# The last batch's output path as a program of its own, with folded context products

## The reference

```python
# layer 0: 16 heads of width 16
q = ln(x; ln1) @ q_w + q_b;  k = ctx @ k_w + k_b;  v = ctx @ v_w + v_b
hidden = softmax(q k^T / 4, masked) v @ cproj_w + cproj_b + x
y = gelu_tanh(ln(hidden; ln2) @ fc_w + fc_b) @ proj_w + proj_b      # inner width 1024
h = hidden + y
# layer 1: one head of width 256, over the same context
s = (h w_q^T) (ctx w_k^T)^T / 16
out = h + alpha * (softmax(s) (ctx w_v^T)) w_o^T
```

## Time and profile before

| | |
|---|---|
| median of 3 runs | 351.56 us |
| the profiled execution: its time | 353.57 us |
| the profiled execution: span from first to last instruction | 351.8 us |
| busy in the span: PE, DVE, ACT, POOL | 282.2, 217.2, 190.3, 93.0 us |
| iterations of batches 1 and 2 | 67.5 us each |
| iteration of batch 3, up to the last product with the values | 47.8 us |
| from there to the end | 60.3 us |

### The profile page before, as it was taken

One profiled execution on the slowest core, in us unless ns is written; L12 is line 12 of the kernel. 1 busy time (PEld: TensorE's weight loads), 2 busy tenths in 40 slices (PEclk: granted clock), 3 DMA queues, 4 the chain that ended last, 5 costly groups with the idle time before them and its releaser, 6 DMA issues.

```text
span 351.8 us, 5962 instructions
## 1 busy us (share of the span) xinstructions
PE 282.2 (80%) x2053; PEld 202.6 (58%) x2053; DVE 217.2 (62%) x420; ACT 190.3 (54%) x350; POOL 93.0 (26%) x88
## 2 busy tenths in 40 slices
PE   3671869985988998998979899989879888586765
PEld 2450436842336675764856576658467656386654
DVE  4541785466666859876488688665758532627432
ACT  3441264288546587767365959655385862225330
POOL 2152000312100267640022774200237140015200
PEclk9995698788789999999999999999999999967898
DMA  6129993019127107401730190053200000000000
GB/s 188 16 62 182 126 318 107 2 45 132 59 68 122 38 17 112 109 2 46 89 122 0 45 153 26 0 103 61 89 2 1 2 0 2 30 0 2 0 2 30
DMA packets 21485, 22.06 MB, mean 63 GB/s; under 512 B 2388, under 2 KB 18600, under 8 KB 21464
## 3 DMA queue, kind: packets, MB, share of 16 engines
q1 hardware_dynamic: 20024, 18.37, 27.8%
q10 hardware_dynamic: 1440, 3.41, 2.7%
HBM read 11.02 MB, written 1.05 MB: 34 GB/s over the span
## 4 chain that ended last, share of the span: by engine, by line
PE 34%; issue 26%; ACT 11%; POOL 11%; DVE 11%; DMA 4%; SPq 1%; ACTq 0%; POOLq 0%; DVEq 0%
PE post_ps L463 10%; PE post_ps L467 4%; PE om L535 4%; DVE neg_max L1042 3%; PE pre_ps L450 3%; POOL y_l L1343 3%; PE s L508 3%; PE s L525 2%; POOL ft L1338 2%; ACT probs L810 2%; ACT q_stack L801 2%; DMA k_stack<-kp 2%; PE post_ps L586 2%; POOL ln L1283 1%; ACT y_h L824 1%
## 5 line engine op out<-in xcount | busy, mean ns | idle before, releaser
L1042 DVE TENSOR_REDUCE neg_max<-s 128x1 f32<-128x512 f32 x128 | 83.3, 684 | 26.2 <-PE s L508 25.5
L810 ACT ACTIVATE probs<-s 128x512 f32<-128x512 f32 x128 | 75.3, 598 | 29.4 <-PE s L525 28.6
L508 PE MATMUL s<-k_stack,q_stack 97*128 97x512 bf16 x128 | 49.5, 410 | 22.9 <-DMA k_stack<-kp 14.7
L525 PE MATMUL s<-q_stack,k_stack 109*128 109x256 bf16 x256 | 50.5, 281 | 2.9 <-ACT q_stack L801 2.1
L508 PEld LDWEIGHTS s<-k_stack,q_stack 97*128 97x128 bf16 x128 | 12.3, 98 | 49.4 <-DVE neg_max L1042 25.6
L535 PE MATMUL om<-probs,vals 128*17 128x256 f32 x512 | 35.4, 397 | 0.7 <-ACT probs L810 0.7
L525 PEld LDWEIGHTS s<-q_stack,k_stack 109*128 109x128 bf16 x256 | 20.9, 101 | 17.1 <-ACT probs L810 3.8
L1283 POOL TENSOR_TENSOR ln<-ln,minus_half 128x2 f32<-128x2 f32 x8 | 5.6, 704 | 94.3 <-DVE ln L1006 94.3
L1068 DVE TENSOR_TENSOR y_l<-post_ps,y_h 128x512 fp32r<-128x512 f32 x16 | 10.9, 690 | 31.2 <-ACT y_h L824 31.2
L801 ACT ACTIVATE q_stack<-om 13x1024 bf16<-13x1024 bf16 x16 | 16.3, 1017 | 13.7 <-PE om L515 13.4
L824 ACT ACTIVATE y_h<-post_ps 128x512 fp32r<-128x512 f32 x16 | 9.3, 596 | 26.0 <-PE post_ps L467 20.1
(11 more groups left out here) (226 smaller groups left out, 679.9 us busy)
## 6 DMA issues: line engine op xcount, KB each, us to landing
k_stack<-kp SPq DMA_DIRECT2D x48, 128.0 KB
q_stack<-qp SPq DMA_DIRECT2D x48, 64.0 KB
cx<-in_ctx_dram SPq DMA_DIRECT2D x5, 512.0 KB, 6.3
pcx<-in_ctx_dram ACTq DMA_DIRECT2D x3, 512.0 KB, 3.6
xz<-in_x_dram SPq DMA_DIRECT2D x5, 256.0 KB, 5.2
raw_late<-in_L_xattn_fc_w_dram SPq DMA_DIRECT2D x1, 1024.0 KB, 12.4
raw_late<-in_L_xattn_proj_w_dram SPq DMA_DIRECT2D x1, 1024.0 KB, 12.2
h<-in_x_dram ACTq DMA_DIRECT2D x3, 256.0 KB, 2.4
```

The lines of the kernel that those rows point to most:

```text
L508: pe.matmul(s1[:, s % 2, :], q_stack[0:ROW_MAX, hd, chunk(t)], k_stack[0:ROW_MAX, hd, :], start=True, stop=True).then_inc(s1_full, 1)
L525: mm = pe.matmul(s2[:, s % 2, i * LQ:(i + 1) * LQ], k_stack[:, hd, chunk(k)], q_stack[:, hd, :], start=True, stop=True)
L810: act.activation(probs[:, g % 2, s // 2, k:k + 2, :], s2[:, s % 2, :].rearrange("p (k n) -> p k n", k=2), ACT.Exp).then_inc(s2_free, 1)
L1042: dve.tensor_reduce(neg_max[:, g % 2, s % 2, s // 2:s // 2 + 1], s1[:, s % 2, :], AX.X, ALU.max, negate=True).then_inc(s1_free, 1)
```

## The change

The hardware loop over batches 1 and 2 becomes a Python loop, so that all iterations are written out. Batch 2's post table `LATE_AT` is stretched from slots 7 to 37 over slots 7 to 51, and the slots from 39 on lie in the epilogues. The special cases for batch 3 in the post path go away, and `CT0`/`CT1` and the pair `pc` are made for batches 0 to 2 alone. Batch 3 gets its own program (`tail`, `TAIL_AT`), in slots 7 to 66, with six PSUM banks: those of `pre_ps`, `s1`, `s2` and `om`, each used by it only after pre or attention has given it up. It makes from the context of batch 3, which is still there as `cT`, two folded products: `c2` = wa times the transposed context (`C20`, `C21`, after transposes `WTH`, `WTL` of wa), and `cw` = context times wo (`CW0`, `CW1`). With these `S0`/`S1` take h itself and `DL0`/`DL1` the exponentials themselves, and `G` and `PC` fall out. The attention output is transposed group by group (`O0` to `O3`), `NT` and `CP` are split into halves, and so are `HT`, `PT`, `DL` and the store, which SP's queue issues. The second load of the context goes away. GELU works in buffers of its own, one for each chunk (`fx_z`, `ft_z`, over the operands of the attention). The core of the diff, in which steps already described are left out:

```diff
-LATE_AT = {7: "OT", 8: "NT", 9: "CP", 12: "ZT", 13: "F0", 15: "F1", 16: "F2", 18: "PJ0", 19: "F3",
-           21: "PJ1", 22: "CT0", 23: "PJ2", 24: "CT1", 25: "PJ3", 26: "CX", 27: "HT", 28: "G", 29: "S0",
-           31: "S1", 33: "PT0", 34: "PT1", 36: "PC", 37: "DL"}
+LATE_AT = {7: "OT", 10: "NT", 11: "CP", 14: "ZT", 16: "F0", 19: "F1", 22: "F2", 23: "PJ0", 25: "F3",
+           29: "PJ1", 31: "CT0", 32: "PJ2", 33: "CT1", 35: "PJ3", 36: "CX", 37: "HT", 38: "G", 41: "S0",
+           43: "S1", 46: "PT0", 47: "PT1", 48: "PC", 51: "DL"}
...
+TAIL_AT = {7: "WTH", 8: "WTL", 9: "C20", 13: "C21", 17: "CW0", 20: "CW1", 24: "O0", 26: "O1", 28: "N0",
+           31: "O2", 33: "CPa O3", 35: "N1", 36: "CPb", 40: "ZT F0", 41: "F1", 42: "F2", 44: "F3", 45: "PJ0",
+           48: "PJ1 PJ2", 50: "PJ3", 52: "HT0 HT1 S0 S1", 56: "PT0 PT1", 61: "DL0", 66: "DL1"}
+LAST_SLOT = 70
+
+
+TAIL_USES = (("WTH", 0), ("WTL", 0), ("C20", 0), ("C21", 0), ("CW0", 0), ("CW1", 0), ("O0", 1), ("O1", 2),
+             ("N0", 1), ("O2", 2), ("CP", 0), ("O3", 1), ("N1", 2), ("ZT", 3), ("F0", 4), ("F1", 1),
+             ("F2", 2), ("F3", 5), ("H0", 0), ("H1", 5), ("HT0", 3), ("HT1", 4), ("S0", 1), ("S1", 2), ("PT0", 3),
+             ("PT1", 4), ("DL0", 5), ("DL1", 0))
...
+        tail_banks = [pre_ps[:], s1[:, 0, :], s1[:, 1, :], s2[:, 0, :], s2[:, 1, :], om[:]]
...
-            with eng.Fori(1, B - 1) as b:
+            for b in range(1, B - 1):
                 iteration(b, False, False)
...
-                    sp.dma_start(cx[:], ctx[b].rearrange("(p k) d -> p k d", k=TK)).then_inc(last_cx_in, 16)
...
-                sp.wait_ge(h_free, 16 * (B + 1))
+                for t in range(TQ):
+                    bank, count = tail_use(f"DL{t}")
+                    sp.wait_ge(tail_free[bank], count)
+                    sp.dma_start(out[B - 1].rearrange("(p t) d -> p t d", t=TQ)[:, t, :], xz[:, t, :]).then_inc(h_free, 16)
+                sp.wait_ge(h_free, 16 * (B + TQ))
...
+                if step in ("WTH", "WTL"):
+                    o = open_(step)
+                    src = wa["HL".index(step[2])]
+                    for c in range(DC):
+                        for k in range(DC):
+                            mm = pe.transpose(o[:, c * D + k * P:c * D + (k + 1) * P], src[:, k, chunk(c)].bitcast(F32), ident[:])
+                    fill(mm, step)
+                elif step in ("C20", "C21"):
+                    c = int(step[2])
+                    o = open_(step)
+                    ready("WTH")
+                    ready("WTL")
+                    fill(product(o, wt, lambda w, k: w[:, k, chunk(c)], cT, lambda v, k: v[:, k, :], DC), step)
+                elif step in ("CW0", "CW1"):
+                    o = open_(step)
+                    for i in range(2):
+                        t = 2 * int(step[2]) + i
+                        mm = product(o[:, i * D:(i + 1) * D], cT, lambda v, k: v[:, k, chunk(t)], wo, lambda w, k: w[:, k, :], DC)
+                    fill(mm, step)
+                elif step[0] == "O":
+                    g = int(step[1])
+                    o = open_(step)
+                    pe.wait_ge(o_done, NG * (B - 1) + g + 1)
+                    for t in range(TQ):
+                        mm = pe.transpose(o[:, chunk(t)], oT[:, g, chunk(t)], ident[:])
+                    fill(mm, step)
+                elif step in ("N0", "N1"):
+                    c = int(step[1])
+                    o = open_(step)
+                    for g in (2 * c, 2 * c + 1):
+                        ready(f"O{g}")
+                    for t in range(TQ):
+                        mm = pe.transpose(o[:, chunk(t)], z2_z[:, t, chunk(c)], ident[:])
+                    fill(mm, step)
+                elif step in ("CPa", "CPb"):
+                    k = "ab".index(step[2])
+                    o = open_("CP") if k == 0 else tail_banks[tail_use("CP")[0]]
+                    ready_high(f"N{k}")
+                    for t in range(TQ):
+                        for i in range(2):
+                            pe.matmul(o[:, t * D:(t + 1) * D], aT_z[0][:, k, chunk(t)], wc[i][:, k, :],
+                                      start=k == t == i == 0, stop=False)
+                    ready(f"N{k}")
+                    for t in range(TQ):
+                        mm = pe.matmul(o[:, t * D:(t + 1) * D], aT_z[1][:, k, chunk(t)], wc[0][:, k, :], start=False,
+                                       stop=k == t == 1)
+                    if k == 1:
+                        fill(mm, "CP")
...
+                elif step[0] == "S":
+                    t = int(step[1])
+                    o = open_(step)
+                    ready_high(f"HT{t}")
+                    fill(products([(o, lambda v, k: v[:, k, chunk(t)], lambda v, k: v[:, k, :])], aT_z, c2, DC, aT_z,
+                                  lambda: ready(f"HT{t}")), step)
+                elif step[:2] == "PT":
+                    t = int(step[2])
+                    o = open_(step)
+                    ready(f"S{t}")
+                    for k in range(TK):
+                        mm = pe.transpose(o[:, chunk(k)], probs1_z[:, t, chunk(k)], ident[:])
+                    fill(mm, step)
+                elif step[:2] == "DL":
+                    t = int(step[2])
+                    o = open_(step)
+                    ready_high(f"PT{t}")
+                    fill(products([(o[:, 0:D], lambda v, k: v[:, k, chunk(t)], lambda v, k: v[:, k, :])], p1T_z, cw, TK, p1T_z,
+                                  lambda: ready(f"PT{t}")), step)
...
+            def tail_slot(at):
+                for step in tail_steps(at):
+                    tail(step)
+
             def iteration(b, first, last):
                 for at, ab, g, s, attends in slots(b, last):
                     if attends:
@@ -742,6 +914,8 @@
                         pre(b + 1, U_V + V_AT[at])
                     if not first and at in steps_at(b - 1):
                         post(b - 1, steps_at(b - 1)[at])
+                    if last:
+                        tail_slot(at)
                     if first and at in PREP_AT:
                         prepare(PREP_AT[at])
                     if attends:
@@ -751,8 +925,10 @@
                             pv(b, NG - 1, k)
 
             def epilogue():
-                for step in LAST_AT.values():
-                    post(B - 1, step)
+                for at in range(START + NS, LAST_SLOT):
+                    tail_slot(at)
+                    if at in steps_at(B - 2):
+                        post(B - 2, steps_at(B - 2)[at])
...
+                if step == "WTH":
+                    act.activation(wt[0][:].rearrange("p c n -> p (c n)"), full(step), ACT.Copy).then_inc(tail_free[tail_use(step)[0]], 1)
+                elif step in ("C20", "C21"):
+                    high(c2[0][:, int(step[2]), :], full(step))
+                elif step in ("CW0", "CW1"):
+                    i = int(step[2])
+                    if i == 0:
+                        for c in range(2):
+                            act.wait_ge(stacked[c], 16 * STACK_DMAS * B)
+                    high(cw[0][:, 2 * i:2 * i + 2, :].rearrange("p c n -> p (c n)"), full(step))
...
+            def tail_slot(at):
+                for i in tail_chunks(at - GELU_SPLIT):
+                    tail_y_high(i)
+                for step in tail_steps(at):
+                    tail(step)
+                for i in tail_chunks(at - GELU_TANH):
+                    tail_tanh(i)
+                for step in tail_steps(at - 1):
+                    if step in ("S0", "S1"):
+                        tail_exp(int(step[1]))
...
+                elif step == "CPb":
+                    o = full("CP")
+                    dve.wait_ge(tail_xb, 1)
+                    free(dve.tensor_tensor(xz[:].rearrange("p t n -> p (t n)"), o, xz[:].rearrange("p t n -> p (t n)"), ALU.add), "CP")
+                    b, n = tail_use("CP")
+                    dve.wait_ge(tail_free[b], n)
+                    norm_stats(xz, ln1, tail_ln, 0)
...
+            def tail_slot(at):
+                for i in tail_chunks(at - GELU_Y):
+                    dve.wait_ge(tail_th, i + 1)
+                    dve.scalar_tensor_tensor(fx_z[:, i, :], ft_z[:, i, :], 1.0, fx_z[:, i, :], ALU.add, ALU.mult).then_inc(tail_y, 1)
+                for i in tail_chunks(at - GELU_SPLIT):
+                    hi, lo = [t[:, 2 * i:2 * i + 2, :].rearrange("p c n -> p (c n)") for t in y_z]
+                    dve.wait_ge(tail_y_hi, i + 1)
+                    dve.tensor_tensor(lo, fx_z[:, i, :], hi.bitcast(F32), ALU.subtract).then_inc(tail_y_lo, 1)
+                for step in tail_steps(at - 1):
+                    tail(step)
+                if "CPb" in tail_steps(at - 2):
+                    norm_apply(xz, ln1, z2_z, tail_rstd, 0, tail_z2)
+                for i in tail_chunks(at - GELU_CUBE):
+                    dve.wait_ge(tail_square, i + 1)
```

(40 more changed lines are left out.)

274 lines of the change are left out of this document (226 added, 48 removed).

## The result

The changed kernel took 336.0 us (median of 4 runs, 335.6 to 337.57) against 351.6 for the kernel before: a ratio of 0.956, 95% interval 0.952 to 0.959. The forecast was 336.5, from 331 to 343. The total was right, but two stages gained more than their terms said and two less, by about as much. Most of what follows is about that.

What follows compares the result with a forecast made beforehand. PE was taken to bound the middle iterations, a chain the tail. Terms of -0.5, -8.0, +0.9 and -7.5 sum to -15.1 us: 336.7 from the profiled span of 351.8, forecast 336.5 against the median 351.56, range 331 to 343.

Steps and rivals of the forecast that it cites:

- the tail: The 60.3 us behind the last attention, bound by a chain and no engine; forecast to take 45 us instead of 60.
- stage C: Batch 3 from F0 to its last PJ: 20.1 us before, forecast 21.0, so +0.9, with the clock taken as full.
- Stage D: From batch 3's last PJ to the end: 21.7 us before, forecast 14.2, so -7.5; bounds 13 and 16.
- The term for G: In the part from the last PJ to the end: G with its split falls out, 2.4 us.
- Stage B: From the last product with the values to F0 of batch 3: 18.5 us before, forecast 10.5, so -8.0.
- Stage A: The last attention, 243.7 to 291.5 us: PE gets 0.9 us more work, the starting stall mostly goes; forecast -0.5.
- best case of -2.5: Lower bound for the last attention: all of PE's idle 6.7 us halved, -2.5 us.
- the stall at the start: In the last attention: DVE's CP waits for POOL's bias addition and the load of h; idle 0.7 us mostly goes.
- The serial queues: Rival: two programs share in-order queues and hold each other; 357 us if nothing overlapped in the tail; chance 0.04.
- Stage A did not pay: Rival "Stage A pays": batch 3's seven steps in the last attention cost 5.8 us instead of -0.5: 342.5; chance 0.15.
- POOL and VectorE did collide: Rival, F0 to last PJ: each of five POOL operations stretches one DVE operation, 5.4 us, near 341; chance 0.08.
- The larger gain: Rival: the last attention loses its stalls (-2.5), F0 to the last PJ takes PE's 18.1 us: 331.5; chance 0.15.

## Why the prediction was right, and where it wasn't

**The structure held.** The middle iterations kept their length: from `OT` to `OT` they took 67.2 and 66.2 us before (the 67.5 of the table is a window of rows 2, not measured from `OT` to `OT`) and 67.0 to 67.3 and 66.0 written out. The gain lies where it was placed, in the tail: 60.3 us became 48.1. Of the prediction's own signs, PE was busy for 92% of stage C; but F0 came 12.2 us behind the last product and not 10 to 11, the clock in stage C was 0.90, and the tail took 48 us and not 45. **Stage D** came out about as worked out from the earlier trace rows, -8.4 for -7.5. The term for G, 2.4, was measured by itself as 2.6. That PC went is read from the trace alone; its folding was not taken back by itself.

**Stage B** failed in one step, the 0.73 us for the normalization. The prediction had the row that POOL stretches VectorE, and charged it to GELU in stage C, where five POOL operations lie; the one that mattered was POOL's low part of batch 2's context, the longest of all, which the text on stage B does not mention. It ran beside an operation on the critical chain. Without it stage B takes 9.7, 0.8 under the sum's 10.5. The page that was weighed (Trainium skill, GPSIMD Engine Reference, Specifications) names two sorts of VectorE operations that contend, those with two SBUF inputs and those in a two-port mode. The prediction took only the first. The normalization has one tensor input, in SBUF, and took 2.02 us longer beside POOL's 2.35; which mode it ran in no row tells.

**Stage C** failed at "the clock is taken as full, because PE has far fewer gaps". One gap was enough, the 2.32 us that came from stage B, and F0 and F1 took 2.0 us more (297.90 to 302.81, against 296.55 to 299.48 with CX at 34). With the gap gone the stage took 20.7 for the forecast 21.0. The order of the queues cost what was said: PE's S0 to PC and the wide layer fill 18.9 of the 20.7 us.

**Stage A** had two terms mis-sized, and neither by the mechanism named. PE's work was to grow by 0.9 us and fell by 0.5, because the steps that left took 7.5 us of busy time (the kernel with the old table) and were counted as 6.5, and those that came 7.0, counted as 7.4. The idle time was to fall by 1.4 and fell by 2.8. Together that is past the best case of -2.5, which had kept the 0.9 of work. And PE even got a new wait that the text doesn't have, 1.68 us at N0 for VectorE's product with the reciprocals. "PE is already 86% busy" was right for the steps that left, which gave back all of their busy time, and wrong for those that came, 2.8 of whose 7.0 us fell into idle time. Whether the stall at the start cost anything, no run shows; the later slots that were to remove it gained nothing.

**The rivals.** The serial queues did not come: even with batch 2's old table the kernel is 2.7% faster than before, and batch 2's work in stage C costs less than its length. Stage A did not pay (the rival's time should read 342.8: 5.8 for -0.5 is 6.3 more). POOL and VectorE did collide, in stage B once for 2.0 us and in stage C three times for 1.1 us together, not at every POOL operation. The larger gain, 331.5, is what the version with CX moved reaches, but not by the rival's sum: there stage C takes 20.7 and not 18.1, and A, B and D gain 2.5 us more than it says. So the forecast owes its 0.5 us of error to luck: A and D were 3.7 better than said, B and C 3.3 worse.
